# A graph layer's edge pass: edge masks from the one-hot matmul, and one-hots made by VectorE

## Time and profile before

| what | value |
|---|---|
| median of 3 runs | 826.88 us (826.37 to 827.32) |
| span of the profiled execution | 824.3 us |
| PE / DVE / ACT / POOL busy | 655.4 / 588.6 / 532.2 / 589.7 us |
| mean granted clock of TensorE | 0.807 of full |
| moved by DMA | 70.47 MB |

### The profile page before, as it was taken

The page is one execution under the profiler, slowest core; times in us unless marked ns, Lnnn a source line. Parts: engine busy times, 40 slices in busy tenths (PEclk is TensorE's granted clock), DMA queues, the critical chain, the costliest instruction groups (busy, mean ns, idle before and its releaser), DMA issues.

```text
span 824.3 us, 17255 instructions
## 1 busy us (share of the span) xinstructions
PE 655.4 (80%) x4923; PEld 514.2 (62%) x4923; DVE 588.6 (71%) x1960; ACT 532.2 (65%) x1198; POOL 589.7 (72%) x638
## 2 busy tenths in 40 slices
PE   9945677868876776999898888888777988789775
PEld 5734455545543545788777777776666766677654
DVE  4872656586678787778787778775577778777665
ACT  5536888788667755677777767775456656566533
POOL 7437777777777777777777777777777777777760
PEclk9985555565556766799998999999698999889797
DMA  6543223222783233333333333334334444444321
GB/s 189 143 105 74 65 63 67 63 64 66 61 61 67 67 87 78 77 84 79 81 82 77 79 81 80 77 76 108 91 87 104 103 117 124 106 105 102 91 56 33
DMA packets 79478, 70.47 MB, mean 85 GB/s; under 512 B 34040, under 2 KB 65312, under 8 KB 79376
## 3 DMA queue, kind: packets, MB, share of 16 engines
q0 software_dynamic: 19008, 39.88, 24.3%
q1 hardware_dynamic: 60080, 29.28, 13.7%
q10 hardware_dynamic: 288, 0.13, 0.1%
HBM read 62.32 MB, written 6.90 MB: 84 GB/s over the span
## 4 chain that ended last, share of the span: by engine, by line
POOL 49%; issue 19%; PE 14%; DVE 11%; DMA 3%; ACT 1%; DVEq 1%; ACTq 0%; SPq 0%; POOLq 0%
POOL work L1158 49%; PE bank L1286 3%; DMA work<-message_table,src_t 3%; DVE counts L1554 2%; DVE fin L1541 2%; DVE acc L1693 2%; PE bank L537 2%; PE bank L558 2%; PE bank L837 1%; PE bank L546 1%; PE bank L1290 1%; DVE fin L928 1%; PE bank L1324 1%; PE bank L560 1%; DVE stats L949 1%
## 5 line engine op out<-in xcount | busy, mean ns | idle before, releaser
L1158 POOL DMA_INDIRECT work<-message_table,src_t x594 | 565.2, 951 | 192.0 <-issue 178.0
L1286 PE MATMUL bank<-work 128*128 128x144 f32 (+8 forms) x1188 | 250.4, 345 | 71.3 <-DVE acc L1693 67.6
L1286 PEld LDWEIGHTS bank<-work 128*128 128x128 f32 x1188 | 199.6, 236 | 105.3 <-issue 87.1
L1415 ACT ACTIVATE work<-work 128x12 f32<-128x12 f32 (+1 forms) x126 | 26.6, 211 | 153.3 <-DVE work L1662 144.8
L1324 PE MATMUL bank<-work,fin 128*128 128x129 f32 (+1 forms) x882 | 116.8, 289 | 0.0
L1693 DVE TENSOR_TENSOR acc<-acc,bank 128x192 f32 (+8 forms) x297 | 89.2, 300 | 36.7 <-issue 11.5
L1324 PEld LDWEIGHTS bank<-work,fin 128*128 128x128 f32 (+1 forms) x882 | 107.7, 200 | 1.7 <-issue 0.6
L1675 DVE TENSOR_TENSOR work<-bank,work 128x576 f32<-128x576 f32 (+7 forms) x126 | 86.1, 684 | 13.8 <-DVE work L1670 0.9
L1290 PE MATMUL bank<-work 128*4 128x48 f32 (+8 forms) x1188 | 94.6, 206 | 0.0
L1576 DVE SCALAR_TENSOR_TENSOR fin<-bank,counts 128x384 f32<-128x384 f32 (+1 forms) x147 | 81.4, 554 | 14.6 <-ACT bank L1388 13.6
L1388 ACT ACTIVATE bank<-hot_logit 128x384 f32<-128x384 f32 (+1 forms) x147 | 72.7, 494 | 29.4 <-DVE fin L1576 17.7
(11 more groups left out here) (134 smaller groups left out, 743.3 us busy)
## 6 DMA issues: line engine op xcount, KB each, us to landing
work<-message_table,src_t POOLq DMA_INDIRECT x594
side<-near_nodes SPq DMA_DIRECT2D x102, 48.0 KB
side<-logit_parts SPq DMA_DIRECT2D x297, 0.8 KB
message_table<-work SPq DMA_DIRECT2D x12, 262.0 KB, 3.8
work<-message_table SPq DMA_DIRECT2D x48, 65.5 KB
work<-in_x_t SPq DMA_DIRECT2D x12, 256.0 KB, 3.6
fin<-in_x SPq DMA_DIRECT2D x11, 256.0 KB
logits_or_x<-in_x_t SPq DMA_DIRECT2D x11, 256.0 KB, 3.9
```

What stands on the lines that cost most here:

```text
L1158: pool.indirect_dma_start(out=rows_of(n)[:, t, :], out_offset=None, in_=table[:, :], in_offset=bass.IndirectOffsetOnAxis(ap=src_t[:, h, g: ...
L1286: pe.matmul(sums[:, at:at + HEADS * w], rows_here[:, t, 0:P], wt_of(i)[:, t, :], start=h == 0, stop=h == TILES - 1)
```

## The change

- The right-hand side of the one-hot matmul becomes 9 logit parts and, behind them, the first w columns of a 48x48 identity. Its result then holds for each edge the 9 parts and its mask, in PSUM; two banks take turns for it (the bank of the logits and that of the mask). The identities are laid into the ring `q_eye` once, by one ACT copy of 48x20x48 at the start of the prologue.
- `masks` is dropped (126 DVE operations). `weights` reads the mask from that PSUM result. `mask_copy` now copies from PSUM to SBUF (only the matmul for the sums of weights reads it there); it waits for DVE's reduction of the same unit, and stands right before `exps(i+1)` on ACT.
- All one-hots of the first pass are DVE's, one operation for each 512 columns, written over `near` in place; the rings `gap` and `hot` are dropped. A place of `near` is now free once PE has used it (`s_q`), and SP issues its refill two steps later in its list.
- `edge_q(i)` no longer waits for DVE's reduction of unit i-1, but for the weights of unit i-2. The ring of logit parts has 5 places instead of 6.
- `dst_t` is kept for the 94 hot groups only: PE transposes 2 pieces instead of 8, DVE copies 94 columns twice instead of 391.

```diff
-        q_win = upper[:, on:on + n_q].bitcast(bf16).rearrange("p (j q) -> p j q", j=Q_RING)
+        q_eye = side[0:WIN, near_words:near_words + slot_words].bitcast(bf16).rearrange(
+            "p (s c) -> p s c", s=q_slots)
...
+                act.wait_ge(s_const, 4)
+                act.copy(q_eye[:, :, PARTS:PARTS + WIN],
+                         ident[0:WIN, 0:WIN].unsqueeze(1).to_broadcast([WIN, q_slots, WIN])).then_inc(s_eye, 1)
...
             def by_dve(i):
-                return first and HOT_AT <= i - AHEAD < HOT_AT + n_blocks
+                return first
...
+            def from_q(i):
+                n, c = n_tiles(i), PARTS + width(i)
+                return bank[Q_BANKS[i % TWO]][:, 0:n * c].rearrange("p (t c) -> p t c", t=n)
...
                         if taken(i, NEAR) >= 0:
-                            near_used(sp, taken(i, NEAR))
+                            sp.wait_ge(s_q, taken(i, NEAR) + 1)
...
-                        while loaded < n_units and taken(loaded, NEAR) <= at + AHEAD:
+                        while loaded < n_units and taken(loaded, NEAR) <= at + 1:
...
                     def edge_q(i):
                         q_landed(pe, i)
                         one_hot_ready(pe, i)
-                        if i >= 1:
-                            pe.wait_ge(s_qs, i)
+                        if i >= TWO:
+                            pe.wait_ge(s_wt, i - TWO + 1)
                         for t in range(n_tiles(i)):
-                            last = pe.matmul(bank[LOGITS_BANK][:, t * PARTS:(t + 1) * PARTS],
-                                             hot_of(i)[:, t * P:(t + 1) * P],
-                                             q_win[0:WIN, i % Q_RING, t // TILES * PARTS:(t // TILES + 1) * PARTS],
+                            last = pe.matmul(from_q(i)[:, t, :], near_of(i)[:, t * P:(t + 1) * P],
+                                             q_eye[:, slot(i, t // TILES), 0:PARTS + width(i)],
                                              start=True, stop=True)
...
                     def mask_copy(i):
-                        act.wait_ge(s_mask, i + 1)
-                        if i >= 1:
-                            act.wait_ge(s_wt, i)
-                        n = n_tiles(i) * width(i)
-                        act.copy(bank[MASK_BANK][:, 0:n], mask_of(i).rearrange("p t w -> p (t w)")).then_inc(s_mcopy, 1)
+                        act.wait_ge(s_qs, i + 1)
+                        if i >= THREE:
+                            act.wait_ge(s_sum, groups_to(i - THREE))
+                        act.copy(mask_of(i), from_q(i)[:, :, PARTS:PARTS + width(i)]).then_inc(s_mcopy, 1)
...
                         if i + 1 < n_units:
+                            mask_copy(i + 1)
                             exps(i + 1)
...
                     def one_hot(i):
-                        if taken(i, HOTS) >= 0:
-                            dve.wait_ge(s_q, taken(i, HOTS) + 1)
+                        n = len(order[i]) * GROUP
                         near_landed(dve, i)
-                        dve.tensor_scalar(hot_of(i), near_of(i), less_col[0:WIN, 0:1], 0.0, ALU.add, ALU.is_equal).then_inc(s_eq, 1)
+                        for h in range(-(-n // COLS)):
+                            here = near_of(i)[:, h * COLS:min((h + 1) * COLS, n)]
+                            dve.tensor_scalar(here, here, less_col[0:WIN, 0:1], 0.0, ALU.add,
+                                              ALU.is_equal).then_inc(s_eq, 1)
...
-                    def masks(i):
...
-                        dve.tensor_tensor(mask_of(i),
-                                          columns[:, 0:w].unsqueeze(1).to_broadcast([P, n, w]),
-                                          at.unsqueeze(2).to_broadcast([P, n, w]),
-                                          ALU.is_equal).then_inc(s_mask, 1)
```

More of the change, by code:

```diff
@@ L176, in gnn_program @@
         ident = sb("ident", [P, P])
-        columns = sb("columns", [P, WIN])
+        n_columns = max(HOT_WIDTHS)
+        columns = sb("columns", [P, n_columns])
         hot_cols = max(HOT_WIDTHS) * n_blocks
@@ L236, in gnn_program @@
         src_t = sb("src_t", [P, TILES, n_groups], i32)
-        dst_t = sb("dst_t", [P, n_groups, TILES], bf16)
+        dst_t = sb("dst_t", [P, n_hot, TILES], bf16)
         win_col = sb("win_col", [P, n_rows])
@@ L430, in _ @@
                 chain(dve.tensor_copy(less_col[:, :], less_col_i[:, :]))
-                chain(dve.tensor_copy(columns[:, :], columns_i[:, 0:WIN]))
+                chain(dve.tensor_copy(columns[:, :], columns_i[:, 0:n_columns]))
                 dve.tensor_copy(iota16[:, :], columns_i[:, :]).then_inc(s_counts, 1)
@@ L1255, in _ @@
                     last.then_inc(s_ptr, 1)
-                    distances_made(pe, 3)
-                    for h in range(TILES):
-                        for r in range(n_rows):
-                            last = pe.transpose(bank[h][:, r * P:(r + 1) * P],
-                                                dist[:, r, h * P:(h + 1) * P], ident[:, :])
-                        last.then_inc(s_ptr, 1)
-                    prepared(pe, 1 + TILES)
+                    if first:
+                        distances_made(pe, 3)
+                        for h in range(TILES):
+                            pe.transpose(bank[h][:, 0:P], dist[:, 0, h * P:(h + 1) * P],
+                                         ident[:, :]).then_inc(s_ptr, 1)
+                        prepared(pe, 1 + TILES)
+                        pe.wait_ge(s_eye, 1)
                     def edge_q(i):
@@ L1396, in one_hot @@
                         near_landed(act, i)
[L1397 to L1398 removed]
                         for h in range(-(-n // COLS)):
[L1400 to L1405 removed]
+                            here = near_of(i)[:, h * COLS:min((h + 1) * COLS, n)]
+                            act.activation(here, here, ACT.Abs, bias=less_col[0:WIN, 0:1]).then_inc(s_gap, 1)
                             act.wait_ge(s_gap, before + h + 1)
[L1407 to L1408 removed]
+                            act.activation(here, here, ACT.Relu, bias=one_col[0:WIN, 0:1],
+                                           scale=-1.0).then_inc(s_hot, 1)
                     def exps(i):
@@ L1499, in _ @@
                     dve.memset(a_col[:, :, :, HEADS:HEADS + 1], 1.0).then_inc(s_fill, 1)
-                    for h in range(TILES):
-                        dve.wait_ge(s_ptr, 2 + h)
-                        chain(dve.tensor_copy(dst_t[:, :, h], bank[h][:, 0:n_groups]))
                     if first:
+                        for h in range(TILES):
+                            dve.wait_ge(s_ptr, 2 + h)
+                            chain(dve.tensor_copy(dst_t[:, :, h], bank[h][:, 0:n_hot]))
                         at = 0
@@ L1694, in add_sums @@
                                 "p (k w) -> p k w", w=w), ALU.add).then_inc(s_acc, 1)
-                    masks(0)
-                    if n_units > 1:
-                        masks(1)
+                    for i in range(AHEAD):
+                        if by_dve(i):
+                            one_hot(i)
                     logits_of(0)
```

73 lines of the change are left out of this document (20 added, 53 removed).

## The result

| | before | after |
|---|---|---|
| median | 826.85 us (824.6 to 829.0, 20 runs) | 824.94 us (823.7 to 827.0, 20 runs) |
| ratio, 95% interval | | 0.9982 (0.9973 to 0.9990), 1.5 us less |
| a later series (e9 below) | 827.01 us (16 runs) | 824.91 us (11 runs); 0.9978 (0.9968 to 0.9989), 1.8 us less |
| profiled execution: span | 824.3 us | 822.9 us (its own time 826.97 us) |
| first gather, last gather, tail | 54.36, 799.32, 25.0 | 54.24, 800.37, 22.5 |

What follows compares the result with a forecast made beforehand. The prediction took POOL's issue of gathers as the bound. Head 0, gathers -1.4 (masks) + 0.35 (one-hots) and tail 0 gave -1.05 us, from 826.88 to 825.9 us, in a range of 823.7 to 829.5.

Steps and rivals of the forecast that it cites:

- The bound: POOL issues gathers without a pause from 54 to 800 us; work on other engines beside it counts 0.
- The relief of ACT: 200 one-hot passes leave ACT, about 143 us of work, with an effect of 0 on the time.
- The masks' term: Gathers starting inside a DVE mask operation are held until it ends; without masks -1.4 us, bounds 0 and -1.4.
- The one-hots' term: 100 more 16-bit one-hots on DVE lengthen gathers by +0.35 us, from 0.17 us counted for 49.
- Rival 1: Every fast DVE one-hot that covers a gather's start holds it back: net +3.4 us, 830.3 us; chance 10%.
- The doubt that the prediction drew from the counting one-hots: A gather amid DVE's counting one-hots can go unharmed, which speaks against the strict form of the port lock; no size.
- The sum: Head 0, gathers -1.4 + 0.35, tail 0: -1.05 us, from 826.88 to 825.9 us.
- the wrong 2.6 us outside the span: Gap between the profiled span and the median of the runs, used to go from span 823.3 to 825.9 us.
- The tail: The stretch after the last gather, 25.0 us: change 0, at most +0.3 us.
- Rival 3: PE's sums in the tail run at full clock instead of 0.50: -2.2 us, with -1.05 to 823.7; chance 14%.
- DVE as the bound: Count stage: DVE's 9.79 us a unit becomes 10.16, over POOL's 10.01; 842.8 us if one-hots take 0.72; chance 3%.

Runs made afterwards that it cites:

- e9: The changed kernel again, unaltered, beside the kernel before: 824.91 us to 827.01, ratio 0.9978.
- e10: The whole change but the move of the one-hots, which ACT keeps, against the kernel before: 824.20 us, ratio 0.9977.
- e11: The kernel before with its masks kept and all one-hots of the first pass on DVE: 826.76 us, ratio 1.0014.
- e7: The changed kernel with 192 more DVE operations with two SBUF inputs, output unused: 988.44 us, ratio 1.0066 to the kernel before.
- e8: The changed kernel with 192 more DVE operations, one input from PSUM, output unused: 988.35 us, ratio 1.0067 to the kernel before.
- e12: The kernel before with 20 idle matmuls on TensorE (the filler) ahead of its tail: 825.96 us, ratio 0.9998.
- e1 to e4: Masks alone, one-hots alone, filler in the changed kernel, filler in the kernel before: ratios 1.0012, 1.0080, 1.0052, 1.0010 to the kernel before.

## Why the prediction was right or wrong

**The bound: right.** The stream starts at 54.2 to 54.6 in both kernels, has 0.30 before each gather and no wait for sums beyond that. The relief of ACT by 150 us moved nothing that can be measured, as e10 and e11 show. This holds in the condition in which the kernel takes 827 us; at 983 to 994 us the same program has another bound, and no number of the forecast applies.

**The masks' term: right.** Predicted -1.4; their collisions came to 1.38 to 1.48 us in three traces, and taking them out gave -1.9 (-2.7 to -1.0). The mechanism of the earlier trace rows is the one found, and the pair e7 and e8 shows it with one operand's place changed and nothing else.

**The one-hots' term: right in sign, too small.** The step that failed is "beside L1606 I count 0.17 us for 49 ... 100 more make +0.35". The 49 themselves come to 0.23 us in that trace by the count above, and the 100 more measured +0.8 by the traces and +1.2 (0.3 to 2.1) by the medians. So one of the 100 cost twice as much as one of the 49 (8 ns against 4); the likely reason, not shown, is that the 49 stand at a fixed place of the hot stage's step and the others come wherever their step has them. Rival 1 erred the other way, by two assumptions: that any start covered counts, and for half the operation's length. A one-hot counts only if it has run for some 0.09 us and has over 0.12 left, so the cost goes with the square of (0.345 - 0.22), not of 0.345: 0.9 us for 149. The doubt that the prediction drew from the counting one-hots was misplaced: a single one of them is 0.29 us long, and the one that ran into that gather had no more than 0.125 us left; those with 0.2 or more left hold a gather like the others.

**The sum.** -1.4 + 0.8 = -0.6 by the corrected terms, where -1.05 was forecast (taken off the measured median, so the wrong 2.6 us outside the span do no harm); measured are -1.5 (-2.2 to -0.8) and -1.8 (-2.6 to -0.9). Some 1 us of the gain is in no term, so it is luck that the forecast's sum came nearer than the corrected one. The sum of e10 and e11, -0.7 with about 1.3 either way, does not contradict either. Part of the gap between the halves and the whole lies outside the kernel's first and last instruction: e10's device times exceed their spans by 4.2 us (median), all others of the series by 3.9. By the medians of the spans the masks give -2.15, the one-hots +0.6 and the whole change -1.85 (e9), so the halves add up to -1.55, and the remainder is on the side of the masks. Candidates for it are the head (53.3 to 54.6 us in six profiles) and the base length of a gather (median 944 ns in four of them, 947 in e10 and e11), but neither follows the change. This stays open.

**The tail: a rival for the wrong reason.** Rival 3 was written for the case that the change meets a faster tail by luck. It did in the profile. But since the filler moved no median in e12, the profiled execution of before was most likely the odd one, and then 0 was the right term for the median.

**DVE as the bound: rightly held unlikely, at 827 us.** It took 9.75 us for a unit of the count stage, and POOL's gathers 10.0.

## What to carry over

Where GpSimd's issue of gathers is the bound, time on other engines is free as long as it stays hidden, and what matters is the kind of DVE operation: one with an operand from PSUM does not touch a gather (one exception in 1481), one with two SBUF operands (or one of the 16-bit ones here) that already runs when a gather starts holds it until it ends. Its mean cost is (length - 0.16 to 0.22)² / 2 / period, so many short operations are nearly free and one long one is not: moving a mask into a PSUM operand paid, shortening DVE's work would not.

The version that these runs favour has the masks from the matmul and leaves the one-hots on ACT (e10). It is 0.5 us better than the full change at best, which nobody can measure here, but it lost only 0.1% in the other condition, where the one-hots on DVE cost 0.5 to 0.9% more. The filler is not worth its code.

A trace pair shows where two executions differ, not where two kernels do. Here the pair pointed at the tail; medians of kernels with one part changed, and counts over several traces, pointed at the gathers.

## What the runs showed that was not expected

- The wait goes both ways. A one-hot that loses against a gather takes up to 0.59 us instead of 0.34, and it ends at one of two fixed points, 0.32 us after the gather's start or 0.11 after its end. On an engine with time to spare that costs nothing.
- The same chip ran the same kernel at 994 us in one series and at 827 us in another, half an hour later. In the traces of e1 to e4 the gathers kept their 944 ns; 150 to 155 us of POOL's pauses between them and a tail of 42 to 44 us instead of 22 to 25 made the difference, and the mean granted clock was 0.73 instead of 0.81.
- The tail's granted clock can be 0.50 or 1.00 in executions of one kernel; in the 8 us before 803 TensorE was busy for 3.45 us in the trace with 0.50 and for 6.3 to 7.1 in the five with 1.00. That is one trace against five; whether the 20 idle matmuls made the 1.00 of e12 is open, as e11 has it without them.
